# Attention outputs left by feature, scaled in the next stage by inverted sums that transfers spread

## The chip, the cores and the metric

The kernel runs on one core of one Trainium2 chip. The metric is the device time of one execution in microseconds, taken as the median of several runs. The engines are called PE (matmul), DVE (vector), ACT (scalar), POOL (GpSimd) and SP (it only issues transfers here). PSUM is the memory that PE writes its results to, in banks of 512 float32 columns; SBUF is the working memory of 128 partitions. DMA is a transfer; it is moved by some of the core's 16 DMA engines, row by row.

## The reference, cut to what matters

Two transformer layers run over `x` (8 samples, 512 tokens, 320 features), each with self-attention, cross-attention to a context and a gated feed-forward block. The change is in the first layer's self-attention and what follows it:

```python
q = (x @ wq).reshape(b, n, heads, dh).transpose(0, 2, 1, 3)      # 20 heads of 16 features
sim = jnp.einsum('bhid,bhjd->bhij', q, k) * scale
a = jax.nn.softmax(sim, axis=-1)
out = jnp.einsum('bhij,bhjd->bhid', a, v)
out = out.transpose(0, 2, 1, 3).reshape(b, n, heads * dh)
return out @ wo + bo                                              # then x += this, layer norm, q of cross-attention
```

## The kernel before, in words

The kernel is one program of stages, each a block in which every engine has its own instruction list, written out by hand; semaphores (`s[...]`) order the engines among each other. Float32 products are done as three products of high and low parts, so each operand is split: ACT casts the high part, DVE subtracts it to get the low part.

**Self-attention of the first layer** (`self_attention`) works on 40 quads, that is 8 samples by 5 groups of four heads. In iteration `n` of the outer loop PE has eight steps `j`. In each it makes two tiles of scores by query for quad `n + 2` (`natural`, into three banks `nat`), from which DVE takes the maxima (`neg_max`, 16 reductions a quad); two tiles of scores by key for quad `n` (`transposed`, two banks `sT`), which ACT turns into `probs` with Exp; and a part of the products of quad `n - 1` with the values (`products`, into `o_ps`). The values carry a column of ones, so `o_ps` holds for each head 16 rows of outputs by feature, one row with the sum of the probabilities, and unused rows, 32 in all. POOL splits the maxima into three bf16 parts, PE turns them (`turn_shift`, in step 1) and SP spreads them into `q_stack`. In step 4 PE makes two parts of the products.

The output of quad `n - 2` is finished so: ACT copies `o_ps` to `o_sb`, PE turns it by four transposes into an `sT` bank (`turn_output`, L1287, in step 2), ACT copies that to `o_turned` (L1334), DVE inverts the sums (L1385), POOL multiplies (L1352), SP stores `o_nat` to DRAM by token (L1232). Between two quads ACT's copy of `o_ps` is what lets PE begin the next products.

**The dense stage behind it** (`dense_phase(..., 0, "q", ...)`) handles one sample in each turn of a loop over `body`. For the sample two turns ahead it loads the attention outputs (`attn_nat`, five transfers, SP), PE turns them by feature (step `oT`, three tiles of four transposes, L848), ACT and DVE split them (`oT_hi` L949, `oT_lo` L1012), PE projects them (`oproj`, four tiles), DVE adds these to the residual (L1016). For the sample one ahead DVE computes layer norm statistics (`stats`, L1023) and POOL the reciprocal root (L804), DVE normalises (`norm`, `z`), PE turns `z` (`zT`), ACT and DVE split it (`hT_hi` L963, `hT_lo` L1048). For the sample of the turn PE makes the three tiles of `q` in two banks `outp`, ACT and DVE split them (`st_hi` L984, `st_lo` L1070), SP stores them. POOL also splits the weights of a later stage here (L262 to L271).

SP issues transfers in order. In the dense stage it waits until a sample's attention tile is free, issues the loads of the next, and then the stores of a `q`. The second layer has the same dense stage with `by_feature=True`: there the attention outputs lie in DRAM by feature already, are loaded by three transfers into `attn_T`, and the `oT` transposes fall away.

Of the kernel before, what the change touches and what calls it, by code (L numbers as in the profile page):

```python
# [30 lines left out]
P = 128  # L31
# [481 lines left out]
def dense_phase(nc, s, k, layer, main, ln_g, ln_b, ws, wo=None, attn_in=None,  # L513
                ff_bias=None, stores=None, final=None, next_weights=(), by_feature=False, next_bias=None, load=False,
                opening=None):
# [3 lines left out]
    with ExitStack() as ctx:  # L519
# [6 lines left out]

        oT, oproj, zT = ([(x, m) for m in range(n)] for x, n in (("oT", 3), ("oproj", TT), ("zT", 3)))
        items = [] if main == "ff" else [(x, m) for x in main for m in range(TT if x == "v" else 3)]
        if main == "ff":
            ahead = {"oT": 1, "oproj": 1, "stats": 1, "norm": 1, "zT": 1, "tail": -1}  # L530
            between = [[("tail", 0)], oT[0:2], oT[2:], oproj[0:2], oproj[2:], [("stats", 0)], [("norm", 0)],
# [43 lines left out]
        if has_o:  # L575
            attn = sb("attn_T", [P, 3, TOK]) if by_feature else sb("attn_nat", [P, TT, ZCOL])
            n_attn = 3 if by_feature else TT + 1
            oT_hi, oT_lo = sb("oT_hi", [P, 3, TOK], F32R), sb("oT_lo", [P, 3, TOK], F32R)
# [19 lines left out]
        if main == "ff":  # L598
# [3 lines left out]
            "d_const", "attn_in_loaded", "oT_split", "oT_hi_done", "bias2_added", "bn_done",  # L602
# [66 lines left out]
        with nc.Block() as block:  # L669

            @block.sync
            def _(sp):
                def load_attn_T(b, split_b=None):
                    if split_b is not None:
                        sp.wait_ge(s["oT_split"], at["oT_split"] + split_b * 3 + 3)
                    src = rows(attn_in, b * D, D)
# [243 lines left out]
            def _(act):  # L920
# [15 lines left out]
                def step(st, b, r):  # L936
                    kind, m = st
                    if kind == "oT":
                        if not by_feature:
                            bank_full(act, st, b)  # L940
                        elif m == 0:
# [48 lines left out]
            def _(dve):  # L990
# [14 lines left out]
                def step(st, b, r):  # L1005
                    kind, m = st
                    if kind == "oT":
# [91 lines left out]
        for name, n in {  # L1099
                "d_const": 16 * n_const, "attn_in_loaded": 16 * n_attn * BATCH if o else 0, "oT_split": 3 * BATCH * by_feature, **{g + x: n * BATCH for g, n in groups.items() for x in ("_full", "_drained")},  # L1100
# [19 lines left out]
def self_attention(nc, s, k, q, kk, v, out, next_weights, bias):  # L1120
# [8 lines left out]
    with ExitStack() as ctx:  # L1129
        def sb(name, shape, dt=F32):  # L1130
# [10 lines left out]
        recip = sb("recip", [P, 2, TT, 4])  # L1141
        o_sb, o_turned = sb("o_sb", [P, TOK]), sb("o_turned", [P, 2, TOK])
        o_nat = sb("o_nat", [P, 2, TT, 4, DH])
# [9 lines left out]
            "a_turn_full", "a_turn_free", "a_pv_done", "a_o_copied", "a_o_normed", "a_recip",  # L1153
# [11 lines left out]
        for n in range(-1, NQ + 2):  # L1165
            for j in range(UNITS):
# [4 lines left out]
                if exists(n - 2) and j == 2:  # L1171
# [1511 lines left out]
```

## Time and profile before

| | us |
|---|---|
| median of 3 runs | 3342.19 |
| lowest and highest | 3334.15, 3347.52 |
| profiled execution | 3342.7 |
| its span, first to last instruction | 3341.0 |
| self-attention of the first layer | from 207 to 699 |
| the dense stage behind it | from 702 to about 851 |

The busy time of an engine says how much of a stretch it worked. A wait is read from the idle time ahead of an instruction and from what released it, in square brackets. [...] "DMA" in a row of stretches is the mean busy share of the 16 DMA engines, which can pass 1 where an engine has several rows in flight.

### The profile page before, as it was taken

How to read it: one execution, taken by the hardware profiler on the slowest of the kernel's cores; microseconds unless marked ns; L12 is line 12 of the kernel's file. 1: busy time of each engine (PE TensorE's matmuls, PEld its weight loads, DVE VectorE, ACT ScalarE, POOL GpSimd, SP SyncE). 2: the span in 40 equal slices, each digit the busy share in tenths (PEclk: the TensorE clock that was granted, in tenths of full speed). 3: DMA queues.
4: the chain of work that ended last, by engine and by line, in shares of the span. 5: the costliest groups of instructions: out<-in, count | busy, mean ns of one | idle time of the engine just before them, and what ended most of it. 6: DMA issues, size and time to landing. Idle time of an engine off the chain costs nothing. (4 is left out here: it accounts for less than half of the span.)

```text
span 3341.0 us, 47964 instructions
## 1 busy us (share of the span) xinstructions
PE 2936.9 (88%) x15594; PEld 1775.7 (53%) x15594; DVE 2157.7 (65%) x3834; ACT 1892.4 (57%) x3214; POOL 805.5 (24%) x1149
## 2 busy tenths in 40 slices
PE   6989999978696999998959999879978577899999
PEld 5754444457455888886731111111126342788888
DVE  5668888837453444444649999968868685444443
ACT  4328888844353232233549999989975355333322
POOL 2021221114640000000027888200003471200000
PEclk9969999989798999998975555555559898899999
DMA  8663333336762000001567557266723213010000
GB/s 228 211 166 101 106 107 103 90 80 158 165 176 46 10 10 19 9 0 38 152 173 163 128 137 164 32 90 83 97 56 96 79 45 92 26 36 18 25 17 16
DMA packets 358243, 296.57 MB, mean 89 GB/s; under 512 B 175602, under 2 KB 281914, under 8 KB 358058
## 3 DMA queue, kind: packets, MB, share of 16 engines
q1 hardware_dynamic: 347994, 273.93, 34.0%
q0 software_dynamic: 7280, 18.07, 2.1%
q10 hardware_dynamic: 2784, 2.29, 0.4%
q8 instruction: 94, 1.54, 0.2%
q14 instruction: 91, 0.75, 0.1%
HBM read 177.53 MB, written 114.52 MB: 87 GB/s over the span
## 5 line engine op out<-in xcount | busy, mean ns | idle before, releaser
L1591 PE MATMUL nat<-k_stack,q_stack 48*128 48x512 bf16 x640 | 381.0, 605 | 71.5 <-DMA k_stack<-k1w 31.1
L1391 DVE TENSOR_REDUCE neg_max<-nat 128x1 f32<-128x512 f32 x640 | 400.7, 682 | 61.3 <-PE nat L1250 61.2
L1625 DVE TENSOR_REDUCE m_all<-nat 128x1 f32<-128x512 f32 x640 | 423.3, 691 | 18.1 <-PE nat L1591 17.8
L804 POOL TENSOR_TENSOR rstd<-var_eps,neghalf 128x4 f32<-128x4 f32 x48 | 51.9, 1081 | 1588.0 <-DVE var_eps L1028 1588.0
L1645 ACT ACTIVATE nat<-nat,m_all 128x512 f32<-128x512 f32 x640 | 427.7, 2130 | 3.0 <-DVE m_all L1625 2.9
L1645 ACT ACTIVATION_READ_ACCUMULATOR nat<-nat,m_all 128x1 f32 x640 | 403.6, 1674 | 0.0
L1054 DVE SCALAR_TENSOR_TENSOR ff<-outp,bias,gel 128x512 f32<-128x512 f32 x160 | 120.1, 751 | 417.6 <-PE outp L326 417.6
L1325 ACT ACTIVATE probs<-sT 128x1024 f32<-128x1024 f32 x320 | 328.0, 1027 | 93.1 <-PE sT L1259 85.5
L968 ACT ACTIVATE gel<-outp,bias 128x512 f32<-128x512 f32 x160 | 110.0, 688 | 351.6 <-PE outp L326 351.6
L1839 ACT ACTIVATE exps<-sT 128x1024 f32<-128x1024 f32 x320 | 293.4, 1573 | 10.5 <-PE sT L1788 10.5
L972 ACT CAST ff_hi<-ff 128x512 fp32r<-128x512 f32 x160 | 99.2, 620 | 312.3 <-DVE ff L1054 312.3
L1591 PEld LDWEIGHTS nat<-k_stack,q_stack 48*128 48x128 bf16 x640 | 64.1, 102 | 387.9 <-ACT nat L1645 350.8
L1876 DVE TENSOR_SCALAR probs<-exps 128x1024 bf16<-128x1024 f32 x320 | 218.3, 692 | 67.8 <-ACT exps L1839 67.8
L1788 PE MATMUL sT<-q_stack,k_stack 51*128 51x512 bf16 x640 | 194.2, 604 | 34.6 <-DMA q_stack<-shift_rows 12.2
L1250 PE MATMUL nat<-k_stack,q_stack 48*128 48x512 f32 x640 | 200.8, 524 | 20.1 <-DMA k_stack<-k_hi 11.7
L1277 PE MATMUL o_ps<-probs,v_stack 128*32 128x256 f32 x2560 | 199.8, 394 | 1.1 <-issue 1.1
L1057 DVE TENSOR_TENSOR ff_lo<-ff,ff_hi 128x512 fp32r<-128x512 f32 x160 | 122.1, 763 | 109.7 <-ACT ff_hi L972 109.7
L1048 DVE TENSOR_TENSOR hT_lo<-h,hT_hi 128x512 fp32r<-128x512 f32 x144 | 111.6, 780 | 106.0 <-ACT hT_hi L963 105.7
L1250 PEld LDWEIGHTS nat<-k_stack,q_stack 48*128 48x128 f32 x640 | 80.0, 193 | 163.6 <-DVE neg_max L1391 129.2
L1259 PE MATMUL sT<-q_stack,k_stack 51*128 51x512 f32 x640 | 157.7, 430 | 0.5 <-ACT probs L1325 0.2
L1788 PEld LDWEIGHTS sT<-q_stack,k_stack 51*128 51x128 bf16 x640 | 34.0, 102 | 184.0 <-ACT exps L1839 165.7
L326 PE MATMUL outp<-hT_hi,Wff_hi 128*128 128x512 f32 x320 | 125.9, 393 | 4.6 <-DVE hT_lo L1048 4.6
(561 smaller groups left out, 7163.3 us busy)
## 6 DMA issues: line engine op xcount, KB each, us to landing
v<-vpad SPq DMA_DIRECT2D x64, 320.0 KB, 2.8
q_stack<-q_part SPq DMA_DIRECT2D x90, 160.0 KB, 5.8
k_stack<-k1w SPq DMA_DIRECT2D x90, 160.0 KB, 10.5
q_stack<-q_hi SPq DMA_DIRECT2D x160, 64.0 KB, 2.5
v_stack<-v SPq DMA_DIRECT2D x40, 256.0 KB, 3.2
q_stack<-q_hi SPq DMA_DIRECT2D x80, 128.0 KB, 2.8
raw<-v SPq DMA_DIRECT2D x16, 640.0 KB, 14.9
k_stack<-k_hi SPq DMA_DIRECT2D x158, 64.0 KB, 2.2
```

The source lines that it names most:

```text
L326: mm = pe.matmul(out, stay, move, start=(n == 0), stop=(n == len(terms) - 1))
L1250: pe.matmul(nat[(16 * n + t) % 3][:, :], q_stack[half, n % RING, pr, qt * P:(qt + 1) * P], k_stack[half, n % RING, pr, :], start=True, sto ...
L1259: mm = pe.matmul(sT[use % 2][:, ab, :], k_stack[half, n % RING, pr, kt * P:(kt + 1) * P], q_stack[half, n % RING, pr, :], start=True, stop ...
L1277: mm = pe.matmul(o_ps[VCOL * h:VCOL * h + VCOL, tok], v_stack[:, n % 2, kt, VCOL * h:VCOL * h + VCOL], probs[:, n % 2, h, kt, tok], start= ...
L1325: act.activation(probs[:, n % 2, 2 * pr:2 * pr + 2, kt, :], sT[use % 2][:, :, :], ACT.Exp, scale=DH ** -0.5).then_inc(s["a_turn_free"], 1)
L1391: dve.tensor_reduce(neg_max[:, n % 2, qt, 2 * pr + ab:2 * pr + ab + 1], nat[(16 * (n + 2) + t) % 3][:, :], AX.X, ALU.max, negate=True).the ...
L1591: pe.matmul(bank[i % NAT][:, :], q_stack[half, slot, g, pr, qt * P:(qt + 1) * P], k_stack[half, slot, g, pr, :], start=True, stop=True).th ...
L1625: dve.tensor_reduce(k.m_all[:, column(i // TILES, i % TILES)], bank[i % NAT][:, :], AX.X, ALU.max, negate=True).then_inc(s["e_max_ready"], 1)
L1645: act.activation(b[:, :], b[:, :], ACT.Exp, bias=k.m_all[:, col], accum_out=k.s_all[:, col]).then_inc(s["a_nat_free"], 1)
L1788: mm = pe.matmul(sT[u % TURNS][:, ab, :], k_stack[half, slot, g, pr, kt * P:(kt + 1) * P], q_stack[half, slot, g, pr, :], start=True, stop ...
L1839: act.activation(exps[:, u % EXPS], sT[u % TURNS][:, :, :], ACT.Exp).then_inc(s["a_turn_free"], 1)
L1876: dve.tensor_scalar(probs[:, u % KEPT], exps[:, u % EXPS], ROUND, -ROUND, ALU.add, ALU.add).then_inc(s["e_rounded"], 1)
```

## The change

In self-attention the output of a quad is stored as it stands, 128 rows (four heads of 32 rows) by 512 tokens: ACT's copy goes to one of two `o_sb`, and SP stores it. PE's four transposes, ACT's second copy, DVE's small reciprocal and POOL's multiplication are gone. Once for each sample SP loads its 20 rows of sums as 80 rows of 128, DVE inverts them at its ninth reduction of a quad, and SP stores the inverted sums (`self_shares`, 20 rows of 512).

In the dense stage the five loads of a sample are replaced by eight. Four bring the outputs by feature, from sources of 8, 8, 4 and 4 heads by 16 rows by 512 tokens; four bring the inverted sums, each head's row repeated 16 times. DVE multiplies the two tile by tile (step `scale`, three tiles, three turns ahead), then ACT and DVE split the product out of SBUF. PE's twelve transposes a sample are gone.

```diff
         elif has_o:
             ahead = {"oT": 2, "oproj": 2, "stats": 1, "norm": 1, "double": 1, "zT": 1}
+            if scale:
+                ahead["scale"] = 3
             body = [("stats", 0), *oT[0:2], items[0], oT[2], ("norm", 0), items[1], items[2], oproj[0], ("double", 0),
-                    zT[0], zT[1], oproj[1], zT[2], oproj[2], oproj[3]]
+                    zT[0], zT[1], oproj[1], zT[2], *scale[0:2], oproj[2], *scale[2:], oproj[3]]
...
                 def load_attn_T(b, split_b=None):
                     if split_b is not None:
                         sp.wait_ge(s["oT_split"], at["oT_split"] + split_b * 3 + 3)
+                    if scale:
+                        heads = rows(attn_in, b * (QUADS * P), QUADS * P).rearrange("(h c) t -> h c t", c=VCOL)[:, 0:DH, :]
+                        spread = rows(recips, b * HEADS, HEADS).unsqueeze(1).broadcast_to([HEADS, DH, TOK])
+                        for tile, src in ((attn, heads), (shares, spread)):
+                            for c in range(2):
+                                sp.dma_start(tile[:, c, :], src[8 * c:8 * c + 8]).then_inc(s["attn_in_loaded"], 16)
+                            for half in range(2):
+                                sp.dma_start(tile[64 * half:64 * half + 64, 2, :], src[16:HEADS]
+                                             ).then_inc(s["attn_in_loaded"], 16)
+                        return
...
+                    if kind == "scale":
+                        if m == 0:
+                            dve.wait_ge(s["attn_in_loaded"],
+                                        at["attn_in_loaded"] + b * (16 * n_attn) + 16 * n_attn)
+                        dve.tensor_tensor(attn[:, m, :], attn[:, m, :], shares[:, m, :], ALU.mult
+                                          ).then_inc(s["o_scaled"], 1)
...
+                def load_sums(b):
+                    for r in range(2):
+                        wait(sp, f"a_o_stored{r}", 16 * ((QUADS * (b + 1) - r + 1) // 2))
+                    sums_of = rows(out, b * (QUADS * P), QUADS * P).rearrange("(h c) t -> h c t", c=VCOL)[:, DH, :]
+                    sp.dma_start(sums[:, :], sums_of.rearrange("h (x t) -> h x t", t=P)
+                                 ).then_inc(s["a_sums_loaded"], 16)
+                def store_shares(b):
+                    wait(sp, "a_recip", b + 1)
+                    sp.dma_start(rows(recips, b * HEADS, HEADS).rearrange("h (x t) -> h x t", t=P), shares[:, :]
+                                 ).then_inc(s["a_recip_stored"], 16)
...
-                    if exists(n - 3):
-                        wait(sp, "a_o_normed", n - 2)
-                        sp.dma_start(rows(out, (n - 3) * TOK, TOK).rearrange("(t p) c -> p t c", p=P),
-                                     o_nat[:, (n - 3) % 2].rearrange("p t h c -> p t (h c)")
-                                     ).then_inc(s[f"a_o_stored{(n - 3) % 2}"], 16)
+                    if exists(n - 2):
+                        wait(sp, "a_o_copied", n - 1)
+                        sp.dma_start(rows(out, (n - 2) * P, P), o_sb[:, n % 2, :]).then_inc(s[f"a_o_stored{n % 2}"], 16)
+                    if exists(n - 3) and (n - 3) % QUADS == QUADS - 1:
+                        load_sums((n - 3) // QUADS)
+                    if exists(n - 4) and (n - 4) % QUADS == QUADS - 1:
+                        store_shares((n - 4) // QUADS)
...
-                        if exists(n - 2) and j == 2:
-                            turn_output(n - 2)
...
-                        wait(act, "a_turn_full", output_use(n - 3) + 1 if n > 2 else 0)
-                        act.copy(o_sb[:, :], o_ps[:, :]).then_inc(s["a_o_copied"], 1)
+                        wait(act, f"a_o_stored{n % 2}", 16 * (n // 2 - 1))
+                        act.copy(o_sb[:, n % 2, :], o_ps[:, :]).then_inc(s["a_o_copied"], 1)
...
-                            act.copy(o_turned[:, n % 2, :], output_bank(n - 2)).then_inc(s["a_turn_free"], 1)
...
-                    pool.tensor_tensor(o_nat[:, r], o[:, :, :, 0:DH],
-                                       recip[:, r].unsqueeze(3).broadcast_to([P, TT, 4, DH]), ALU.mult
-                                       ).then_inc(s["a_o_normed"], 1)
...
+                def invert(b):
+                    wait(dve, "a_sums_loaded", 16 * (b + 1))
+                    wait(dve, "a_recip_stored", 16 * b)
+                    dve.reciprocal(shares[:, :], sums[:, :]).then_inc(s["a_recip"], 1)
...
+                        if t == 8 and exists(n - 4) and (n - 4) % QUADS == QUADS - 1:
+                            invert((n - 4) // QUADS)
...
             dense_phase(nc, s, k, 0, "q", w["n2_g"], w["n2_b"], [wq], wo, self_out, stores={"q": q20},
-                        next_weights=[w1])
+                        next_weights=[w1], by_feature=True, recips=self_shares)
```

What stood on PE around step 2 of a quad of self-attention before (`turn_output` is L1287, `products` L1277):

```order
L1259 MATMUL sT_175<-q_stack,k_stack 128x512 x2
L1287 MATMUL sT_176<-ident,o_sb 128x128 x4
L1277 MATMUL o_ps<-probs,v_stack 32x256 x4
L1250 MATMUL nat_173<-k_stack,q_stack 128x512
L1250 MATMUL nat_174<-k_stack,q_stack 128x512
L1259 MATMUL sT_175<-q_stack,k_stack 128x512 x2
```

And now, with the line numbers of the changed kernel:

```order
L1278 MATMUL nat_173<-k_stack,q_stack 128x512
L1278 MATMUL nat_174<-k_stack,q_stack 128x512
L1287 MATMUL sT_176<-q_stack,k_stack 128x512 x2
L1305 MATMUL o_ps<-probs,v_stack 32x256 x4
L1278 MATMUL nat_172<-k_stack,q_stack 128x512
```

The four transposes are gone, and the products follow the scores directly, as in every other step.

On DVE in the dense stage one turn of the loop stood so before, from the third `oT_lo` to the next statistics:

```order
L1012 TENSOR_TENSOR oT_lo<-oT_223,oT_hi 128x512
L1034 TENSOR_SCALAR z<-x_resid,mv,rstd 128x320 x4
L1016 TENSOR_TENSOR x_resid<-x_resid,oproj_224 128x320
L1048 TENSOR_TENSOR hT_lo<-h_214,hT_hi 128x512 x2
L1016 TENSOR_TENSOR x_resid<-x_resid,oproj_225 128x320
L1048 TENSOR_TENSOR hT_lo<-h_214,hT_hi 128x512
```

And now, from the normalisation of the same turn to its end:

```order
L1057 TENSOR_SCALAR z<-x_resid,mv,rstd 128x320 x4
L1039 TENSOR_TENSOR x_resid<-x_resid,oproj_224 128x320
L1071 TENSOR_TENSOR hT_lo<-h_215,hT_hi 128x512 x2
L1039 TENSOR_TENSOR x_resid<-x_resid,oproj_225 128x320
L1071 TENSOR_TENSOR hT_lo<-h_215,hT_hi 128x512
L1028 TENSOR_TENSOR attn_T<-attn_T,shares 128x512 x2
L1039 TENSOR_TENSOR x_resid<-x_resid,oproj_224 128x320
L1028 TENSOR_TENSOR attn_T<-attn_T,shares 128x512
L1039 TENSOR_TENSOR x_resid<-x_resid,oproj_225 128x320
```

Three multiplications (L1028) have come between the last `hT_lo` and the last two additions, behind which the next statistics stand.

On SP at the start of the dense stage the loads of the first sample now stand so:

```order
L686 DMA attn_T<-self_out 128x1x512 x2
L688 DMA attn_T<-self_out 64x1x512 x2
L686 DMA shares<-self_shares 128x1x512 x2
L688 DMA shares<-self_shares 64x1x512 x2
```

They are the eight transfers; the first multiplication of a sample waits for all of them.

## Rows read from the trace of the kernel before

**Rows 1.** Stretches: PE, PEld, DVE, ACT, POOL busy (instructions), PEclk, DMA share, GB/s.
```profile
264.00:650.00 386.00, 376.00 (x3466) 158.64 (x3464) 337.84 (x569) 317.39 (x369) 75.62 (x198) 1.00 0.38 105
701.00:830.00 129.00, 104.96 (x595) 89.15 (x596) 89.19 (x195) 55.67 (x92) 44.24 (x58) 0.91 0.56 137
```

**Rows 2.** Timeline, DVE in one quad: start, us, instruction, idle before and releaser.
```profile
404.29 2.42 DVE L1391 TENSOR_REDUCE neg_max<-nat 128x1 f32<-128x512 f32 x4
407.03 1.29 DVE L1391 TENSOR_REDUCE neg_max<-nat 128x1 f32<-128x512 f32 x2 [0.31 <-PE nat L1250]
409.04 2.53 DVE L1391 TENSOR_REDUCE neg_max<-nat 128x1 f32<-128x512 f32 x4 [0.72 <-PE nat L1250]
411.97 3.81 DVE L1391 TENSOR_REDUCE neg_max<-nat 128x1 f32<-128x512 f32 x6 [0.41 <-PE nat L1250]
415.70 0.24 DVE L1385 RECIPROCAL recip<-o_turned 128x16 f32<-128x16 f32 x1
```

**Rows 3.** Timeline, PE in steps 1 to 3 of the same quad.
```profile
405.75 0.33 PE L1267 MATMUL sT<-identb,parts 128*32 128x128 bf16 x3
...
407.38 0.63 PE L1287 MATMUL sT<-ident,o_sb 128*128 128x128 f32 x4
...
408.50 0.50 PE L1250 MATMUL nat<-k_stack,q_stack 48*128 48x512 f32 x2
```

**Rows 4.** Groups of instructions: count, busy us, mean ns, idle before.
```profile
L1012 DVE TENSOR_TENSOR oT_lo<-attn_T,oT_hi 128x512 fp32r<-128x512 f32 x48 | 31.3, 685 | 13.9 <-ACT oT_hi L949 13.9
...
L1385 DVE RECIPROCAL recip<-o_turned 128x16 f32<-128x16 f32 x40 | 9.8, 245 | 27.0 <-ACT o_turned L1334 27.0
...
L2334 DVE RECIPROCAL inv_step<-step 128x3 f32<-128x3 f32 x1 | 0.2, 177 | 0.0
```

**Rows 5.** Timeline, end of self-attention and start of the dense stage.
```profile
696.41 0.59 ACT L1318 COPY o_sb<-o_ps 128x512 f32<-128x512 f32 x1 [2.60 <-PE o_ps L1277]
...
701.84 2.09 SPq L691 DMA_DIRECT2D attn_nat<-self_out  x4
...
707.40 1.97 PE L848 MATMUL oT<-ident,attn_nat 128*128 128x128 f32 x8 [9.70 <-DMA attn_nat<-self_out]
```

**Rows 6.** DMA issues: count, KB each, median us to landing.
```profile
self_out<-o_nat SPq DMA_DIRECT2D x40, 128.0 KB, 2.1
...
k_stack<-q_parts SPq DMA_DIRECT2D x2, 60.0 KB
```

**Rows 7.** Timeline, DVE in the dense stage.
```profile
779.46 0.69 DVE L1048 TENSOR_TENSOR hT_lo<-h,hT_hi 128x512 fp32r<-128x512 f32 x1 [0.25 <-ACT hT_hi L963]
...
781.50 1.67 DVE L1023 BATCH_NORM_STATS2 bn<-x_resid 128x6 f32 x4
...
785.92 0.69 DVE L1012 TENSOR_TENSOR oT_lo<-oT,oT_hi 128x512 fp32r<-128x512 f32 x1 [0.17 <-ACT oT_hi L949]
...
794.83 0.69 DVE L1048 TENSOR_TENSOR hT_lo<-h,hT_hi 128x512 fp32r<-128x512 f32 x1 [0.25 <-ACT hT_hi L963]
...
810.31 0.69 DVE L1048 TENSOR_TENSOR hT_lo<-h,hT_hi 128x512 fp32r<-128x512 f32 x1 [0.24 <-ACT hT_hi L963]
```

**Rows 8.** Stretches of 1 us around SP's two transfers of ones at 1712.56.
```profile
1714.00:1715.00 1.00, 0.00 (x0) 0.00 (x0) 0.13 (x2) 0.00 (x0) 0.00 (x0) 0.50 1.01 415
1719.00:1720.00 1.00, 0.00 (x0) 0.00 (x0) 0.76 (x1) 1.00 (x2) 0.29 (x1) 0.50 0.21 47
1720.00:1721.00 1.00, 0.00 (x0) 0.00 (x0) 0.68 (x2) 0.35 (x1) 1.00 (x1) 0.50 0.21 28
1721.00:1722.00 1.00, 0.00 (x0) 0.00 (x0) 1.00 (x1) 0.00 (x0) 0.89 (x2) 0.50 0.16 33
1722.00:1723.00 1.00, 0.00 (x0) 0.00 (x0) 0.60 (x1) 0.37 (x1) 1.00 (x1) 0.50 0.05 6
```

**Rows 9.** DMA queue from 2520 to 2590: packets, MB, share of 16 engines.
```profile
q1 hardware_dynamic: 4000, 7.21, 33.2%
```

**Rows 10.** Timeline, PE: a gap in the first stage and its clock behind it.
```profile
28.00 0.31 PE L326 MATMUL ctx_a<-v_tail,ctxT_lo 128*128 128x320 f32 x1
31.27 0.73 PE L326 MATMUL ctx_a<-ctxT_hi,Wk_hi 128*128 128x512 f32 x1 [2.97 <-DVE Wk_lo L449]
31.80 0.63 PE L326 MATMUL ctx_a<-ctxT_hi,Wk_lo 128*128 128x512 f32 x1
...
35.50 0.39 PE L326 MATMUL ctx_b<-ctxT_hi,Wk_lo 128*64 128x512 f32 x1
```

More of the change, by code:

```diff
@@ L523, in dense_phase @@
         has_o = wo is not None
+        scale = [("scale", m) for m in range(3)] if recips is not None else []
         oT, oproj, zT = ([(x, m) for m in range(n)] for x, n in (("oT", 3), ("oproj", TT), ("zT", 3)))
@@ L529, in dense_phase @@
         if main == "ff":
-            ahead = {"oT": 1, "oproj": 1, "stats": 1, "norm": 1, "zT": 1, "tail": -1}
-            between = [[("tail", 0)], oT[0:2], oT[2:], oproj[0:2], oproj[2:], [("stats", 0)], [("norm", 0)],
+            ahead = {"oT": 1, "oproj": 1, "stats": 1, "norm": 1, "zT": 1, "tail": -1, "scale": 1}
+            between = [[("tail", 0), *scale], oT[0:2], oT[2:], oproj[0:2], oproj[2:], [("stats", 0)], [("norm", 0)],
                        zT[0:2], zT[2:], []]
@@ L576, in dense_phase @@
             attn = sb("attn_T", [P, 3, TOK]) if by_feature else sb("attn_nat", [P, TT, ZCOL])
-            n_attn = 3 if by_feature else TT + 1
+            n_attn = 8 if scale else 3 if by_feature else TT + 1
+            if scale:
+                shares = sb("shares", [P, 3, TOK])
             oT_hi, oT_lo = sb("oT_hi", [P, 3, TOK], F32R), sb("oT_lo", [P, 3, TOK], F32R)
@@ L940, in step @@
                             bank_full(act, st, b)
+                        elif scale:
+                            act.wait_ge(s["o_scaled"], at["o_scaled"] + b * 3 + m + 1)
                         elif m == 0:
@@ L1220, in _ @@
                 load(1, k_stack, kk, (0, 1, 0))
-                for n in range(-2, NQ + 3):
+                for n in range(-2, NQ + 4):
                     if exists(n + AHEAD):
@@ L1239, in _ @@
                                      ).then_inc(s[f"a_v_loaded{(n + 1) % 2}"], 16)
-                for r in range(2):
-                    wait(sp, f"a_o_stored{r}", 16 * (NQ // 2))
+                wait(sp, "a_recip_stored", 16 * BATCH)
             @block.tensor
@@ L1281, in products @@
                         mm.then_inc(s["a_pv_done"], 1)
-                def turn_output(n):
-                    wait(pe, "a_o_copied", n + 1)
-                    wait(pe, "a_turn_free", output_use(n) - 1)
-                    for qt in range(TT):
-                        mm = pe.transpose(output_bank(n)[:, qt * P:(qt + 1) * P], o_sb[:, qt * P:(qt + 1) * P],
-                                          k.ident[:, :])
-                    mm.then_inc(s["a_turn_full"], 1)
                 PRODUCTS = {1: (0,), 2: (1,), 3: (2,), 4: (3, 4), 5: (5,), 6: (6,), 7: (7,)}
@@ L1371, in _ @@
                         early.add(pool, n)
-                for n in range(NQ - 4, NQ):
-                    norm(n)
             @block.vector
@@ L1379, in _ @@
                 dve.memset(words(k_stack[0:64, 1:, :, :]), 1.0).then_inc(s["a_rows_set"], 1)
[L1380 to L1385 removed]
+                def invert(b):
+                    wait(dve, "a_sums_loaded", 16 * (b + 1))
+                    wait(dve, "a_recip_stored", 16 * b)
+                    dve.reciprocal(shares[:, :], sums[:, :]).then_inc(s["a_recip"], 1)
+                for n in range(-2, NQ + 4):
+                    if not exists(n + 2) and exists(n - 4) and (n - 4) % QUADS == QUADS - 1:
+                        invert((n - 4) // QUADS)
                     for t in range(16 if exists(n + 2) else 0):
```

49 lines of the change are left out of this document (14 added, 35 removed).

## The prediction

> **What bounds the kernel now.** I read the stretches first [rows 1], then the order in time inside one quad and one sample, then the transfers. In self-attention PEclk is 1.00, PE is busy 376.00 of 386.00 us and DVE 337.84. PE looks like the bound, but its busy time counts overlapping matmuls, so the waits decide. 569 DVE instructions at 17 a quad are 33.5 quads, 11.5 us each. One quad on DVE [rows 2] is sixteen reductions, 2.42 + 1.29 + 2.53 + 3.81 = 10.05 us, and three waits for PE's `nat`: 0.31, 0.72 and 0.41. The whole runs in a ring: a reduction frees a bank, PE fills it. DVE is the fuller side, and what PE does beside the scores shows as DVE's waits. The 0.31 stands behind `turn_shift` (405.75), the 0.72 behind the four transposes of `turn_output` (407.38) [rows 3].
>
> In the dense stage one sample takes 810.31 - 794.83 = 15.5 and 794.83 - 779.46 = 15.4 us [rows 7], and DVE is busy 89.19 of 129 us, PE 104.96, DMA 0.56 [rows 1]. DVE waits little at the places shown (0.25, 0.17). So PE and DVE share the pace and the transfers are not late. That last point is what the change puts at risk.
>
> **Removed in self-attention.** PE's slot of `turn_output` runs from 407.38 to the next `nat`; the four transposes take 0.63 with their tail, about 0.55 in issue. Without them the 0.72 wait falls to 0.15, what a wait with scores alone in front would keep. That is -0.57; the bound above is all 0.72 and a little of the wait behind it, -0.75; below, -0.4, if `turn_shift`'s place then ends last. I take -0.65 in each of the 36 quads in full swing: -23.4. The last four, where the ring runs out, give PE's 0.63 each: -2.5. ACT's second copy, POOL's multiplication and DVE's small reciprocal (245 ns, 40 of them [rows 4]) are worth nothing more: ACT is busy 317 and POOL 76 of 386 us [rows 1], and the reciprocal at 415.70 lies in time that the parts chain takes before `turn_shift` can start. If that cover is gone, it is another -0.2 a quad, -7 in all, and I keep that as an outer bound.
>
> **Added in self-attention.** Seven reciprocals of 80x128 come at DVE's ninth reduction, and an eighth at the end. No row shows that shape. Two do show the operation: 245 ns for 16 elements and 177 for 3 [rows 4], 5.2 ns an element, so 128 elements take 177 + 125 x 5.2 = 0.83 us. From below it costs 0 (it fits into the 0.41 wait before `nat` at 411.97), from above 0.9. I take 0.83 - 0.41, rounded up to 0.5, times 7: +3.5.
>
> [...]
>
> SP has one store for one store in each quad (256 KB for the 128 KB of [rows 6]), and once a sample two small transfers behind it. Each wait on SP stands before the `v` load of the next quad, which has a quad's time to land; I cost that at nothing, and at 1 us a sample if not.
>
> At the end of the stage a chain grows. Today ACT's copy ends at 697.0, and the first dense load stands at 701.84 [rows 5]: turn, scale, store. Now it is copy 697.0, store 2.1, load of sums 2.1, reciprocal 0.95 with its waits, store of shares 2.1, all at the 2.1 us to landing of [rows 6], and 0.65 of waits between: 704.9, +3.05. Bounds +1 and +5.
>
> Self-attention: -23.4 - 2.5 + 3.5 + 3.0 = -19.4, with -26 and -14 as bounds.
>
> **The dense stage, DVE's part.** Today the end of the last `hT_lo` (780.15) and the end of the third `oT_lo` (786.61) are 6.46 us apart [rows 7]: two additions, statistics (1.67), splits. Now three multiplications stand in between. They have the shape of `oT_lo`, 685 ns [rows 4], 2.06 together; about 0.6 of it fills DVE's waits for the two additions. So 6.46 + 1.45 = 7.9 us from the first multiplication to the end of the third `oT_lo`. PE's twelve transposes (0.25 us each by 1.97 for eight [rows 5]) go, 3 us a sample, which opens PE's side.
>
> **The loads.** SP may load sample b+1 only at the end of the third `oT_lo` of sample b, since `attn` is one buffer. Then the load runs, then the three multiplications. So period = 7.9 + load. To stay within the pace of today the load must take under 16.05 - 7.9 = 8.1 us. It is eight transfers, 768 rows of 2 KB.
>
> What a 2 KB row costs on an engine: from 2520 to 2590 q1 moved 4000 packets and 7.21 MB at 33.2% of 16 engines [rows 9], 0.332 x 16 x 70 / 4000 = 93 ns. Spread over 16 engines, a load is 48 rows on each: 4.5 + 2.1 of fixed time [rows 6] = 6.6 us, which is hidden.
>
> Whether they spread is the question. Nearly all transfers of before have an outermost count of 16, 64 or 128 on both sides. One sizable kind has not: the two of ones from `q_parts`, three heads by 20 rows of 1 KB, 60 KB each [rows 6]. Around them [rows 8] the share is 1.01 and 415 GB/s where everything runs, and then 0.21, 0.21 and 0.16 with 28 to 47 GB/s over more than three microseconds, until they are in. Three of sixteen is 0.19. Both transfers sat on the same three engines, with 2 x 20 = 40 rows on each, about 3.4 us, 85 ns a row. So an outermost count of 3 gave three engines, and the second transfer did not choose others.
>
> [...]
>
> From the rows alone: if count 3 gives three engines, counts 8, 8, 4, 4 for `attn` and again for `shares` give 8 and 4, all starting with the same one. A transfer of 128 rows on 8 engines is 16 rows on each, one of 64 rows on 4 engines also 16. The first four engines carry all eight: 128 rows x 93 ns = 11.9 us, and 2.1 fixed: 14.0 us a load. From below 128 x 85 = 10.9 + 1.0; from above the engines also carry the stores of q and the loads of `w1`.
>
> The period is then 7.9 + 14.0 = 21.9 us. With t0 the stage's start: sample 0 is multiplied at t0 + 14.0, sample 1 at 31.8 (split in 3.8, load 14.0), sample 2 at 53.1, and five periods of 21.9 later sample 7 at 162.6. Its place today is the end of `hT_lo` of sample 5, 811.0, with t0 = 701.84 that is 109.2 [rows 5, 7]. The difference is +53.4. About 0.6 more comes from what is left behind it: **+54**. Bounds: load 12 us gives 15 less in all, +39, and +30 if half of DVE's additions also fall into the load's time; load 16 gives +68.
>
> PE will wait some 9 us in each sample, and its clock will fall: behind a gap of 2.97 us it ran 512-column matmuls 0.53 us apart (0.63 each) and only later at 0.39 each [rows 10]. PE's work of a sample, 104.96 x 15.4 / 129 = 12.5, less 3 for the transposes, is 9.5; 0.63/0.39 times that is 15.3, under 21.9. So a low clock is covered while the loads set the pace, and costs a few us only in the last turns. That is inside the bounds.
>
> **The sum.** 3342.7 (the profiled execution, within 0.6 of the median 3342.19) - 19.4 + 54 = 3377.3.
>
> **Rivals.**
> - **The loads spread over all engines, and the clock holds.** Then the load is 6.6 us and hidden, DVE sets the pace: +1.45 a turn less 0.8 that it waits elsewhere now, +0.65 x 6 = +4, and +1.5 at the start (sixteen-engine loads replace the one at 701.84, and multiplication goes ahead of the split). 3342.7 - 19.4 + 5.5 = 3329, not slower. For it: 48 rows an engine, and that a single kind of transfer is the witness against. Against it: the share of 0.21 [rows 8]. It decides if a load takes under 8.1 us, which needs about 65 rows or fewer on the fullest engine.
> - **The same, and the clock falls.** Without transposes PE has 9.5 us of work in 15.4, and the q tile that waits for a bank until DVE has done the additions leaves a gap of up to 2.9 us, as long as the one of [rows 10] behind which the matmuls took 0.63 instead of 0.39. PE's work is then 15.3 in 16.0, and some of it shows: +1.0 x 8. 3329 + 8 = 3337.
> - **The forecast's mechanism, and the engines are also full otherwise.** The DMA share in this stage is 0.56 today [rows 1]; much is the short rows that go. If 0.2 of it stays on the first four engines, 11.9 becomes 14.9, +3 x 7 = +21: 3398, and over 3404 with the low clock uncovered.
> - **Self-attention doesn't speed up,** because `turn_shift` or POOL's parts take over the 0.72. Then only -0.2 a quad is left, and each case above is 16 higher. I hold it for one in ten and have put it into the ranges.
>
> **Chances.** Forecast 0.64, with its own range 3356 to 3402; fuller engines 0.06; loads spread, clock holds 0.16 (3320 to 3336); loads spread, clock falls 0.14 (3330 to 3345). Half a per cent, 17 us, is about what a measurement here can tell from no change: faster is under 3325, slower over 3359. Faster holds a third of the third case, 0.06; same the rest of it, the last case, and the low end of the first, 0.26; slower 0.68. The range is 3329 to 3404.
>
> **What would show it.** Right: DVE's `attn_T` multiplication waits for a DMA, near 6 us in each sample; the dense stage's period is about 22 us; the DMA share is 0.25 to 0.5 while a load runs and nothing else does; SP's eight transfers land some 14 us after issue. In self-attention the wait of 0.72 is about 0.15 and a quad takes 10.9; the 80x128 reciprocal takes 0.8. Wrong: a dense period of 16, a load in 7 us with a share near 1, or multiplications that wait for nothing; then the time is below 3340. A quad still at 11.5 would say that the transposes cost nothing.

## The result and the profile after

The changed kernel takes 3388.22 us (median of 4, 3384.85 to 3391.06) where the one before takes 3344.86 in runs beside it: a ratio of 1.0134, 95% interval 1.0107 to 1.0161. The forecast was 3377 with a range of 3329 to 3404. It is slower, by the mechanism that was forecast, and by 11 us more than was said. Of all executions that are reported below, one (of the version `fm_pool`) took 3977.54 us at a mean granted clock of 0.61, where its others have 0.84, and it is left out of that version's ratio.

**Self-attention** did speed up. DVE in its quads, to be held against [rows 2] (start, us, instruction, idle before and its releaser):

```profile
399.06 6.31 DVE L1393 TENSOR_REDUCE neg_max<-nat 128x1 f32<-128x512 f32 x10 [0.41 <-PE nat L1278]
405.67 3.86 DVE L1393 TENSOR_REDUCE neg_max<-nat 128x1 f32<-128x512 f32 x6 [0.30 <-PE nat L1278]
409.95 6.32 DVE L1393 TENSOR_REDUCE neg_max<-nat 128x1 f32<-128x512 f32 x10 [0.41 <-PE nat L1278]
416.57 3.85 DVE L1393 TENSOR_REDUCE neg_max<-nat 128x1 f32<-128x512 f32 x6 [0.30 <-PE nat L1278]
```

A quad takes 416.57 - 405.67 = 10.90 us, where it took 11.57. The waits of 0.31 and 0.41 stand as before, the one of 0.72 is gone altogether. The same stretches as in [rows 1], and two from a load beside which no other transfer runs (PE, PEld, DVE, ACT, POOL busy, PEclk, DMA share, GB/s; PEclk is the granted clock of TensorE as a share of its full speed):

```profile
264.00:650.00 386.00, 376.30 (x3518) 152.53 (x3514) 355.48 (x563) 317.92 (x353) 54.63 (x167) 1.00 0.41 119
701.00:830.00 129.00, 71.12 (x333) 57.56 (x332) 72.95 (x147) 38.87 (x66) 32.49 (x40) 0.76 0.40 127
697.00:703.00 6.00, 4.06 (x26) 3.80 (x24) 0.97 (x2) 0.00 (x0) 0.00 (x0) 0.94 0.50 161
703.00:707.00 4.00, 0.00 (x0) 0.00 (x0) 0.00 (x0) 0.00 (x0) 0.00 (x0) 0.69 0.27 98
```

DVE's share of self-attention rose from 337.84 to 355.48 us of 386, since its waits went. In the same 129 us of the dense stage everything fell: PE from 104.96 to 71.12, DVE from 89.19 to 72.95, the DMA share from 0.56 to 0.40. No engine is the bound any more. The load itself has two parts: first the 16 DMA engines are busy for 0.50 at 161 GB/s, the share of eight of sixteen, and then for 0.27 at 98 GB/s, near the 0.25 of four of sixteen, while no other engine works.

The end of self-attention, to be held against [rows 5] (SP's and DVE's timeline):

```profile
669.36 0.33 SPq L1259 DMA_DIRECT2D self_out<-o_sb  x1
671.45 0.86 SPq L1234 DMA_DIRECT2D sums<-self_out  x1
673.94 0.95 DVE L1383 RECIPROCAL shares<-sums 80x128 f32<-80x128 f32 x1 [29.45 <-DMA sums<-self_out]
674.91 0.34 SPq L1239 DMA_DIRECT2D self_shares<-shares  x1
676.83 1.34 SPq L686 DMA_DIRECT2D attn_T<-self_out  x2
```

The four links (store, load of the sums, reciprocal, store of the inverted sums) are there one behind the other, 7.5 us from the end of ACT's copy at 669.33 to the first dense load. That load stands 25.0 us earlier than before (701.84).

The dense stage, to be held against [rows 7]: DVE's timeline around one sample, then SP's.

```profile
750.37 0.69 DVE L1071 TENSOR_TENSOR hT_lo<-h,hT_hi 128x512 fp32r<-128x512 f32 x1 [0.25 <-ACT hT_hi L980]
756.21 1.29 DVE L1028 TENSOR_TENSOR attn_T<-attn_T,shares 128x512 f32<-128x512 f32 x2 [5.14 <-DMA shares<-self_shares]
757.82 0.69 DVE L1028 TENSOR_TENSOR attn_T<-attn_T,shares 128x512 f32<-128x512 f32 x1
759.05 1.67 DVE L1046 BATCH_NORM_STATS2 bn<-x_resid 128x6 f32 x4 [0.15 <-DVE x_resid L1039]
763.22 0.93 DVE L1035 TENSOR_TENSOR oT_lo<-attn_T,oT_hi 128x512 fp32r<-128x512 f32 x1
779.30 1.29 DVE L1028 TENSOR_TENSOR attn_T<-attn_T,shares 128x512 f32<-128x512 f32 x2 [4.56 <-DMA shares<-self_shares]
```

```profile
740.87 1.44 SPq L686 DMA_DIRECT2D attn_T<-self_out  x2
...
764.34 1.58 SPq L686 DMA_DIRECT2D attn_T<-self_out  x2
```

From the first multiplication (756.21) to the end of the third `oT_lo` (764.15) it is 7.94 us; from there to the next load 0.2; the load is 15.0 (764.34 to 779.30). Before a sample's first multiplication DVE idles 4.6 to 7.9 us in the last six samples, and 16.1 and 9.7 us in the first two. POOL's `rstd`, once a sample, gives the period, 23.8 us for the first one shown:

```profile
714.27 1.42 POOL L819 TENSOR_TENSOR rstd<-var_eps,neghalf 128x4 f32<-128x4 f32 x1 [69.40 <-DVE var_eps L1051]
738.05 1.46 POOL L819 TENSOR_TENSOR rstd<-var_eps,neghalf 128x4 f32<-128x4 f32 x1 [20.51 <-DVE var_eps L1051]
...
855.33 1.41 POOL L819 TENSOR_TENSOR rstd<-var_eps,neghalf 128x4 f32<-128x4 f32 x1 [15.12 <-DVE var_eps L1051]
871.39 1.04 POOL L819 TENSOR_TENSOR rstd<-var_eps,neghalf 128x4 f32<-128x4 f32 x1 [8.64 <-DVE var_eps L1051]
```

Six periods from 714.27 to 855.33 are 23.5 us each, the last, with no load left, 16.1. Before, the last `rstd` of the stage stood at:

```profile
830.22 1.04 POOL L804 TENSOR_TENSOR rstd<-var_eps,neghalf 128x4 f32<-128x4 f32 x1 [8.34 <-DVE var_eps L1028]
```

From first load to last `rstd` the stage took 830.22 - 701.84 = 128.4 us and takes 871.39 - 676.83 = 194.6: +66.2. With the 25.0 of self-attention that is +41.2 of the span's +45.0 (3341.0 to 3386.0). The other 3.8 lie behind this last `rstd`, 0.6 of them up to the next stage; single executions of one kernel differ by more (3334 to 3349 before).

### The profile page after: what moved, and what is told of

It reads as the page before. It is cut to its first block and busy times, and to the rows that moved or that the text cites. A ratio compares the mean times of both kernels' runs of the same rounds, so it can differ in the third digit from the quotient of the medians.

```text
span 3386.0 us, 47173 instructions
## 1 busy us (share of the span) xinstructions
PE 2913.9 (86%) x15338; PEld 1754.9 (52%) x15338; DVE 2179.6 (64%) x3826; ACT 1873.2 (55%) x3174; POOL 785.1 (23%) x1109
## 5 line engine op out<-in xcount | busy, mean ns | idle before, releaser
L1844 ACT ACTIVATE exps<-sT 128x1024 f32<-128x1024 f32 x320 | 293.4, 1567 | 10.6 <-PE sT L1793 10.6
L1287 PE MATMUL sT<-q_stack,k_stack 51*128 51x512 f32 x640 | 159.0, 431 | 0.5 <-ACT probs L1343 0.2
## 6 DMA issues: line engine op xcount, KB each, us to landing
k_stack<-k1w SPq DMA_DIRECT2D x90, 160.0 KB, 10.8
raw<-v SPq DMA_DIRECT2D x16, 640.0 KB, 14.5
```

Of the source, the lines that this page charges most:

```text
L1287: mm = pe.matmul(sT[use % 2][:, ab, :], k_stack[half, n % RING, pr, kt * P:(kt + 1) * P], q_stack[half, n % RING, pr, :], start=True, stop ...
L1844: act.activation(exps[:, u % EXPS], sT[u % TURNS][:, :, :], ACT.Exp).then_inc(s["a_turn_free"], 1)
```

## The experiments

**Does the load last as long as its rows on the fullest engine?** The edits here and below are cut to what matters. First the suspected cost is enlarged: the same bytes go in twelve transfers of four heads.

```diff
-for c in range(2):
-    sp.dma_start(tile[:, c, :], src[8 * c:8 * c + 8])
+for c in range(4):
+    sp.dma_start(tile[64 * (c % 2):64 * (c % 2) + 64, c // 2, :], src[4 * c:4 * c + 4])
```

> The changed kernel with the same bytes loaded in twelve transfers of four heads each, none of eight. Theory (a source whose outermost count is 4 goes to four engines, always the same ones): 12 x 16 = 192 rows of 2 KB on each of them, 17.9 + 2.1 = 20 us alone instead of 14.2, 21.3 beside other transfers instead of 15.5; 8 loads x 5.8 = 46 more: 3388 + 46 = 3434, between 3425 and 3445. DMA share while a load runs alone 0.25 instead of 0.34. Rival (the load is as long as SP needs to issue it, or as all its bytes take): twelve issues of 0.64 us are 7.7, still under 14, the load stays at 14.2: 3388 to 3395.

3426.39 us, ratio 1.0249 (1.0231 to 1.0266). The first load ran from SP's issue at 675.90 to the multiplication at 695.26 (its DVE row, and a stretch from the middle of the second, beside which no other transfer ran):

```profile
695.26 1.90 DVE L1029 TENSOR_TENSOR attn_T<-attn_T,shares 128x512 f32<-128x512 f32 x3 [21.31 <-DMA shares<-self_shares]
```

```profile
705.00:711.00 6.00, 1.59 (x11) 1.32 (x10) 0.00 (x0) 0.00 (x0) 0.00 (x0) 1.00 0.26 98
```

That is 19.4 us instead of 14.2 with not one byte more. The share is 0.26 at 98 GB/s, as in the second part of the changed kernel's load; the part at 0.50 is gone. Four of sixteen engines are 0.25. The 64 additional rows on each of these four cost 5.2 us, 81 ns a row. In all it is 38 us more than the changed kernel, where 46 were expected: beside other transfers the load takes 20.0 us in the mean against 15.5, 4.5 more and not 5.8.

Then the same cost taken away. In `feature_major` the features of a tile stand in SBUF in the order feature, head instead of head, feature, so the sources' outermost count is 16; the rows of the output weight are loaded in the same order, and the sum over them is the same.

```diff
-sp.dma_start(tile[:, c, :], src[8 * c:8 * c + 8])
+sp.dma_start(tile[:, c, :], src[8 * c:8 * c + 8].rearrange("h d t -> d h t"))
...
+            return src.rearrange("(h d) n -> d h n", d=DH) if by_feature else src   # the weight's rows
...
+            wo.by_feature = True
```

> The same eight transfers with the same rows and bytes, but features stand in SBUF in the order feature, head (the rows of the output weight are permuted to match), so that the outermost count of every source is 16. Theory (the load is slow because its rows sit on four and eight engines): 48 rows of 2 KB on each of 16 engines, 4.5 + 2.1 = 6.6 us, perhaps 8 beside the stores of q and the weights, so hidden; the dense period falls from 23.5 to about 16.0, 7 x 7.5 = 52 less, the first load 7 less: 3388 - 59 = 3329, between 3322 and 3338. Rival (the loads are slow for what they read: each row of sums read 16 times, heads 64 KB apart): nothing changes, 3388. Rival on the clock: PE's waits leave it at 0.50 in the dense stage, period 17, 3337.

3344.27 us, ratio to before 1.001 (1.0001 to 1.0019), so 44 us less than the changed kernel, against 59 expected, and outside the 3322 to 3338 that were given. The order of the source is the cause: bytes, rows, number of transfers and queue of the load are those of the changed kernel (only POOL's loads of the output weight, in self-attention, are divided otherwise). The 15 missing us have two parts. The load takes 9.6 us in the first sample and 8.5 in the second (SP 690.14, multiplication 698.69), not 6.6, and 9.4 to 10.8 beside others:

```profile
692.00:697.00 5.00, 4.97 (x27) 4.71 (x26) 0.98 (x2) 0.00 (x0) 0.00 (x0) 0.78 1.02 263
```

```profile
698.69 1.29 DVE L1039 TENSOR_TENSOR attn_T<-attn_T,shares 128x512 f32<-128x512 f32 x2 [3.54 <-DMA shares<-self_shares]
...
770.80 1.30 DVE L1039 TENSOR_TENSOR attn_T<-attn_T,shares 128x512 f32<-128x512 f32 x2 [1.22 <-DMA shares<-self_shares]
```

All 16 engines are busy now (1.02), and 263 GB/s over 16 are 125 ns for a row of 2 KB. SP's eight issues of 0.6 us take 5 us of it too (690.14 to 695.18); these runs do not tell the two apart. The other part is the period, 18.1 us where 16.0 was expected, though from the fourth sample on DVE waits for the load 1.2 us or less.

**Is it the exposed part of the load, not the load as such?** `shares_early` keeps four and eight engines but loads the inverted sums as soon as they are used, 5.7 us or so ahead of the outputs:

```diff
-for tile, src in ((attn, heads), (shares, spread)):
+# wait for o_scaled of the sample before
+for tile, src in ((shares, spread), (attn, heads)):
+    if tile is attn and split_b is not None:
+        sp.wait_ge(s["oT_split"], at["oT_split"] + split_b * 3 + 3)
```

> The changed kernel, but SP issues the four loads of the inverted sums first, as soon as the third multiplication of the sample before is done, and only the four of the outputs wait for its third oT_lo. Theory (rows on the fullest engine, exposed behind the third oT_lo): 64 rows are left behind the wait, 64 x 93 ns + 2.1 = 8.1 us, 9 beside other transfers, so the period is 7.9 + 8.1 to 9 = 16 to 17 instead of 23.5: 7 x 7 = 49 less, 3339, between 3331 and 3348. Rival (all engines are the limit, or latency of a load whatever its size): the load is still 14 us behind the third oT_lo, 3385.

3354.36 us, ratio 1.0041 (1.0028 to 1.0055): 34 less than the changed kernel from the order of four transfers alone. From the fourth sample on the wait before a multiplication is 0.9 us or less, and the period falls to 18.2. The 3354 lie outside the 3331 to 3348 that were given. The gain is short of 49 because the loop without any such wait has a slower pace than was thought, as the next run shows.

`fm_early` has both edits.

> feature_major with the inverted sums loaded first, behind the third multiplication, and only the four loads of the outputs behind the third oT_lo. Theory (in feature_major the load was 8.5 us alone and 9.4 to 10.8 beside others, because SP needs 5 us to issue eight transfers, and it was exposed by 0.25 to 1.2 us a sample and 5.6 in the first two): half the transfers behind the wait, load about 6 us, DVE waits for no DMA, period 17.3 instead of 18.1: 3344 - 6 x 0.8 - 4 = 3335. Rival (PE at its low clock sets the pace and the wait for the load only hid it): no gain, 3343.

3335.08 us, ratio 0.998 (0.9971 to 0.9989), as expected to a tenth. From the third sample on DVE waits for no transfer, and the period is 17.1. That is the price of the multiplications on DVE with what they bring along (PE's low clock, below): 1.7 us a sample over the 15.4 of before, where the prediction had 0.65.

**What is the scaling worth in all?** `no_scale` neither loads the inverted sums nor multiplies, so the output is left unnormalised; the outputs still come from 8, 8, 4, 4 heads.

```diff
-scale = [("scale", m) for m in range(3)] if recips is not None else []
+scale = []
-for tile, src in ((attn, heads), (shares, spread)):
+for tile, src in ((attn, heads),):
```

> The changed kernel without its scaling: the inverted sums are neither loaded nor multiplied in the dense stage (the output is left unnormalised), the four loads of the outputs stay at 8, 8, 4, 4 heads. Theory: 64 rows on the fullest engine, 8.1 us a load; DVE's part is 6.5 again, so 14.8, below the 15.4 of the pace before: period about 15.4, the first load 6 shorter, 3388 - 7 x 8.1 - 6 = 3325, between 3317 and 3332. Rival (one such load by itself is slow, however many rows): period stays over 20, 3370 and more.

3320.41 us, ratio 0.9932 (0.9917 to 0.9948), period 15.3. Half the rows on the same four engines are hidden in the steady loop: DVE waits for no transfer from 700 us on. The rival that such a load is slow by itself, with a period over 20, is refuted.

**Where does PE's low clock come from, and is it the pace?** In `feature_major` and `fm_early` the rival on the clock has come true. PE's timeline of `fm_early` (at the gap) and of `shares_early`, where the same gap stands:

```profile
754.38 0.69 PE L336 MATMUL outp<-hT_hi,q_hi 128*64 128x512 f32 x1 [2.97 <-DVE st_lo L1108]
```

```profile
748.21 0.49 PE L326 MATMUL outp<-hT_hi,q_hi 128*64 128x512 f32 x1 [3.03 <-DVE st_lo L1097]
748.50 0.63 PE L326 MATMUL outp<-hT_hi,q_lo 128*64 128x512 f32 x1
```

Behind the gap a matmul takes 0.63 us, where the 128-wide ones ahead of it take 0.39. The granted clock in `fm_early` is 1.00 from 748 to 751 and 0.52 from 754.8 to 757.5. `fm_first` moves the first `q` tile ahead of the two `oT`:

```diff
-body = [("stats", 0), *oT[0:2], items[0], oT[2], ...
+body = [("stats", 0), items[0], *oT[0:2], oT[2], ...
```

> feature_major with one change in the written order: the first q tile (its products, ACT's st_hi, DVE's st_lo) stands ahead of the first two oT. Theory (PE idles 3.0 us in each sample until DVE has drained the first q tile behind two oT_lo, and its clock falls to 0.50 for the 64-wide tile behind it, 0.63 us a matmul instead of 0.39): the gap becomes 1.8 us or less, the clock stays at 1.00, the wait for hT falls: about 1 us a sample, 3344 - 7 = 3337. Rival (DVE's chain sets the pace, the gap and the clock are beside it): within 2 us of 3344.

3351.32 us, ratio 1.0022 (1.0013 to 1.0031), 7 us slower than `feature_major`, which neither the theory nor its rival gives. The part of the theory on the clock held: from the second such gap on it is 1.6 to 2.0 us, and the matmuls behind it take 0.39.

```profile
742.76 0.45 PE L336 MATMUL outp<-hT_hi,q_hi 128*64 128x512 f32 x1 [1.73 <-DVE st_lo L1105]
743.05 0.39 PE L336 MATMUL outp<-hT_hi,q_lo 128*64 128x512 f32 x1
...
749.37 1.23 PE L875 MATMUL zT<-ident,z 128*128 128x128 f32 x8 [3.12 <-DVE z L1069]
```

```profile
744.69 4.55 DVE L1069 TENSOR_SCALAR z<-x_resid,mv,rstd 128x320 f32 x4
```

Behind a gap of 1.73 us the matmuls take 0.39. What that is worth can't be read from the total, since the four `z` on DVE (the normalised rows) now take 4.55 us instead of 3.08 in `feature_major`, PE waits 3.12 for them, and the period is about 19. Why `z` is slower there I did not settle; POOL's weight split falls beside it, but that is so in the kernel before too, where the four take 2.66.

**Can the multiplications leave DVE's chain?** `fm_pool` is `fm_early` with them on POOL, behind its split of the weights.

```diff
+                        if b + 2 < BATCH:
+                            for st in scale:
+                                step(st, b + 2, b % 2)       # pool.tensor_tensor(attn, attn, shares, mult)
```

> fm_early with the three multiplications on POOL, behind its split of the weights, instead of DVE. Theory (DVE's chain is the pace, the 2.06 us of multiplications stand in it whole, and one rstd beside DVE costs little): POOL needs about 1.4 us for each (860 ns for 128x320), beside DVE; the period falls to 15.4 to 15.8 and the time to 3335 - 6 x 1.7 = 3325. Rival (POOL and DVE slow each other when both read SBUF, as z went from 2.66 to 3.08 us and rstd from 1.04 to 1.46): multiplications of 2 us and more, oT_hi late, period 17 or more, 3335 or above.

3326.13 us, ratio 0.9948 (0.9935 to 0.9961): this version is faster than both kernels. The period is 15.2 (its `rstd` at 750.15, 765.36, 780.59), about as before the change. DVE waits for the first `hT` of a sample 0.79 instead of 1.33, and the granted clock from 720 to 795 is 0.98:

```profile
720.00:795.00 75.00, 62.23 (x337) 50.13 (x338) 61.99 (x124) 38.18 (x63) 54.83 (x60) 0.98 0.81 226
```

```profile
758.14 0.69 DVE L1095 TENSOR_TENSOR hT_lo<-h,hT_hi 128x512 fp32r<-128x512 f32 x1 [0.80 <-ACT hT_hi L1008]
```

**Self-attention: what were the transposes worth?** In the kernel before, done twice:

```diff
-for qt in range(TT):
+for qt in [*range(TT), *range(TT)]:
     mm = pe.transpose(output_bank(n)[:, qt * P:(qt + 1) * P], ...
```

> The kernel before, with the four transposes of turn_output done twice over in each quad. Theory (they stand in the ring of DVE and PE and show one to one as a wait of DVE): DVE's wait of 0.72 becomes about 1.3, 36 x 0.55 + 4 x 0.6 = 22 more, 3367 beside 3345, between 3360 and 3372. Rival (the wait belongs to POOL's parts or to turn_shift, the transposes are free): 3345.

3360.98 us, ratio 1.0059 (1.0044 to 1.0075), 19 more where 22 were expected. The one wait grew and no other:

```profile
412.67 2.53 DVE L1391 TENSOR_REDUCE neg_max<-nat 128x1 f32<-128x512 f32 x4 [1.16 <-PE nat L1250]
415.61 3.81 DVE L1391 TENSOR_REDUCE neg_max<-nat 128x1 f32<-128x512 f32 x6 [0.41 <-PE nat L1250]
```

0.72 became 1.16. 0.44 in each of 40 quads are 17.6 of the 19. So the transposes stood on the path; a wait that belonged to POOL's parts or to `turn_shift` would not have grown.

**And the reciprocals and sums?** `recip_x3` makes each reciprocal three times, two of them into unused tiles.

```diff
+for i in range(2):
+    dve.reciprocal(spare[:, 2 * b + i, :], sums[:, :])
 dve.reciprocal(shares[:, :], sums[:, :]).then_inc(s["a_recip"], 1)
```

> The changed kernel with each of the eight 80x128 reciprocals made three times (the extra ones into tiles that nobody reads). Theory (one reciprocal of 0.94 is nearly covered, three quads with one of them took 33.0 instead of 3 x 10.90, so 0.3 shows; the cover is the 0.41 wait, and what goes beyond it shows whole): 1.88 - 0.1 more in each of 7 quads and 1.9 at the end: 3388 + 14 = 3402, between 3397 and 3406. Rival (DVE has slack in every quad, PE sets the pace): 3390 to 3392.

3423.82 us, ratio 1.0249 (1.0234 to 1.0264), 36 more, not 14. The wait itself is as expected: the two quads around the first one (313.10 to 336.76) take 23.66, 1.86 over 2 x 10.90. But PE idles meanwhile, and in three of the seven its clock falls. DVE's timeline, its waits for PE and two stretches at the second of them:

```profile
379.26 1.75 DVE L1385 RECIPROCAL spare<-sums 80x128 f32<-80x128 f32 x2
380.93 0.89 DVE L1386 RECIPROCAL shares<-sums 80x128 f32<-80x128 f32 x1
...
391.87 1.29 DVE L1396 TENSOR_REDUCE neg_max<-nat 128x1 f32<-128x512 f32 x2 [1.63 <-PE nat L1279]
394.03 1.29 DVE L1396 TENSOR_REDUCE neg_max<-nat 128x1 f32<-128x512 f32 x2 [0.87 <-PE nat L1279]
```

```profile
376.00:386.00 10.00, 8.61 (x76) 3.25 (x78) 9.09 (x14) 5.46 (x7) 0.00 (x0) 0.88 0.30 91
386.00:396.00 10.00, 10.00 (x56) 3.85 (x52) 5.87 (x10) 6.12 (x7) 1.75 (x5) 0.50 0.29 84
```

At 0.50 PE is the slower side of the ring, and DVE waits 0.87 and 1.63 where it waited 0.30. The three quads from 369.47 to 409.30 take 39.83 us instead of 3 x 10.90, 7.1 more, and the three around each of the other two falls 8.6 more. So a stall of 1.9 us cost about four times itself there.

`no_sums` leaves out the loading, inverting and storing of sums; the dense stage loads rows of the outputs as its second factor, so the output is wrong by that.

> The changed kernel without the path of the sums in self-attention: they are not loaded, inverted or stored, and the dense stage loads its second factor from rows of the outputs instead, in the same eight transfers (the output is wrong by that). Theory (the path is nearly covered inside the stage, 0.3 us in each of 7 quads, and stands whole behind the last quad: load of sums 2.5, reciprocal 0.95, store 1.9): 2.1 + 5.4 = 7.5 less, 3381, between 3377 and 3385. Rival (DVE's seven reciprocals cost the 0.5 us each that the prediction gave them, and the transfers of sums hold up SP): 3376 or less.

3386.92 us (3377.42 to 3393.9), ratio 1.012 (1.010 to 1.014). In its trace the first dense load stands at 668.00, 8.8 earlier, a little more than the 7.5 expected. The total does not show it: the first load there took 15.1 us instead of 14.2, the last `rstd` is 4.5 earlier, and its profiled run is longer behind that. As a time this run is inconclusive. The place of the first load doesn't decide either: 0.5 us a reciprocal instead of 0.3 would make it 8.9 instead of 7.5, and in the eight traces that have this path unchanged the place itself lies between 675.55 and 678.19. What the trace does show is the path behind the last quad: from the end of ACT's last copy to the first dense load it is 2.6 us instead of 7.5. What the path costs within the stage stays open.

## Why the prediction was right, and where it was off

- **Engines of a load: right.** The counts 8, 8, 4, 4 put 128 rows on four engines. 14.0 us was said for a load, 14.16 and 14.24 measured for the first two, beside which nothing else of size ran; `by_four` and `feature_major` moved it to 19.4 and 8.5 by the outermost counts. The trace of before had shown one such count, 3 with a share of 0.21 to 0.16 [rows 8]; that 8 would give eight engines and 4 four was my estimate from it. The shares agree with it: 0.50 and then 0.27 for the counts 8 and 4, 0.26 for 4, 1.02 for 16. What other counts give was not measured. That the four engines are the same ones each time is read from the time of a load, 14.2 us for 128 rows and 19.4 for 192, which is that of all their rows one behind the other; which engines they are no view here shows. One bound was loosely founded: 85 ns was the price of a row of 1 KB [rows 6, 8], taken for one of 2 KB, which then cost 81.
- **DVE's part: right.** 7.9 said, 7.94 measured. (The prediction puts sample 2 at 53.1, where its own 31.8 and 21.9 give 53.7; nothing hangs on it.)
- **The load beside others: the term that was off.** The prediction kept 14.0 for all eight loads and put the rest into the bounds. The six later ones took 14.5 to 16.6, 15.5 in the mean. In the second load q1 was the only queue; in the third POOL's weights moved beside it on q0, and later the stores of `q` as well. That this traffic is what lengthens the load was not tried by a run of its own. The answers on the DMA queues from 695 to 709 and from 716 to 733 (packets, MB, share):

```profile
q1 hardware_dynamic: 816, 1.57, 34.3%
```

```profile
q1 hardware_dynamic: 816, 1.57, 29.4%
q0 software_dynamic: 144, 0.49, 13.2%
```

  The period became 23.5 instead of 21.9, and the last multiplication begins 173.2 us behind the first load instead of 162.6: 10.6 of the 12.2 us by which +54 fell short of +66.2. The rest lies between it and the last `rstd`, 21.4 us where it was 19.2 before, 2.2 more and not 0.6.
- **Self-attention: right in kind, 3.3 too small.** -19.4 was said, and the first dense load stands 25.0 us earlier. But 2.3 of the 25.0 lie ahead of this stage: its first reduction already begins at 206.06 instead of 208.33, and the change has no part in what stands before it. That leaves 22.7. The quad gave 0.67 for 0.65. The start of the stage gave 1.6: from the first reduction to the same ten reductions (below) it is 39.9 us instead of 41.6. PE's clock is 0.50 there (225 to 235 in both traces), and it came back earlier in this trace: from 245 to 250 it is 1.00, before it was 0.52. It isn't a constant of the change: `by_four` and `no_scale`, with the same self-attention, take 41.2 and 41.3.

```profile
249.90 6.34 DVE L1391 TENSOR_REDUCE neg_max<-nat 128x1 f32<-128x512 f32 x10 [1.73 <-PE nat L1250]
```

```profile
245.98 6.30 DVE L1393 TENSOR_REDUCE neg_max<-nat 128x1 f32<-128x512 f32 x10 [0.38 <-PE nat L1278]
```

  The reciprocal took 0.94 where 0.83 was interpolated, and showed about 0.3 a sample instead of 0.5: three quads with one in them, 300.44 to 333.44, took 33.0 for 32.7. The tail grew by 2.7 for 3.05.
- **The sum owes something to luck.** The dense stage was put 12.2 us too low, and what lies ahead of it (with the 2.3 that are no effect of the change) took 5.6 less than was said. The two errors have opposite signs, so that with the 3.8 behind the stage the sum is only 10.4 us short of the profiled execution.
- **The rival with spread loads was mis-sized** by two terms. Its load is 8.5 to 10.8, not 6.6, since a row costs 125 ns rather than 93 with all 16 engines busy; and with the multiplications on DVE the period is 1.7 us above that of before instead of 0.65, even where no load is waited for. `feature_major` makes that rival real: 3344, where 3329 and 3337 were said. Its condition, a load under 8.1 us, was stated right, and not met.
- **The clock:** "a low clock is covered while the loads set the pace" held, since DVE waited for the load in every sample. In `feature_major` the gap before the third `q` tile and the 0.63 behind it came as the second rival described. How much of the 1.7 us it costs there is not shown apart: `fm_first` kept the clock but lengthened `z`, and in `no_scale` and `fm_pool`, with granted clocks of 1.00 and 0.98 from 720 to 795 and periods of 15.3 and 15.2, the multiplications had left DVE as well.

## What to carry to other kernels

Read a transfer's outermost counts before its bytes: this layout change made rows longer and fewer and still put the second part of each load on a quarter of the engines (a share of 0.27 and 14.2 us for counts 8 and 4), and another order of the loops (feature before head, count 16, with the weight's rows to match) brought the share to 1.02 and the load to 8.5 us. Ask then what the load is exposed behind: issuing the half whose buffer comes free early was worth 34 us here without spreading anything. And work added to an engine whose loop is one serial chain can cost nearly its whole length: three multiplications of 2.06 us made the period 1.7 us longer on DVE, and not longer at all on POOL (15.2), which with them was busy for 54.8 of 75 us.

## What the runs showed of the hardware that I had not expected

- A DMA engine's time for a row of 2 KB was the longer the more of them ran: from the GB/s it is 84 ns where the share was 0.26 and 0.27 (98 GB/s over four engines), 102 at 0.50 (161 over eight) and 125 at 1.02 (263 over 16). The load times give 81 for the 64 rows added on four engines, and 94 for a load on eight and four ((14.16 - 2.1) / 128).
- In the gap before the third `q` tile PE idled 2.8 to 5.2 us in every steady sample of `feature_major`, `shares_early` and `fm_early`, and behind it the clock was 0.50 (matmuls of 0.63 for 0.39), in two of them only from the fourth or fifth matmul on. Behind the 16 gaps of 1.27 to 2.08 us there in `no_scale`, `fm_first` and `fm_pool` the matmuls kept 0.39. The first gap of `fm_pool`, 2.51 us, had 0.63 behind it from the fifth matmul on, the first of `fm_first`, 4.87 us, at once. In `recip_x3` three of seven stretches of 2.6 us in which DVE made reciprocals brought 13 to 17 us at the low clock each.
- POOL's `rstd` of 128x4 takes 1.46 us in the changed kernel where it took 1.04, and 1.04 again at the last sample. What differs beside it is DVE's `oT_lo`, which now reads SBUF instead of PSUM and is missing at the last sample. In `fm_first`, where `st_lo` (which reads PSUM) has come ahead of `oT_lo`, `rstd` takes 1.04 again from the second sample on. That points to `oT_lo`; no run changed it alone.
